# Stage three of a four-layer residual kernel: first tiles read and prepared in the last channels of stage two, and a split last store

## The chip, the cores and the metric

One core of a Trainium2 chip runs the whole program. The time is that of the device for one execution, in microseconds (us), as the median of several runs. Smaller is better.

## The reference, cut to what matters

`x` has shape (B, C, T) = (128, 64, 1024), in fp32. Four layers are added to it one after the other:

```python
x = x + conv(x * mask) * mask        # per channel a causal convolution over t with a kernel of 1024 lags;
                                     # mask: t < length[b]
x = x + einsum('bct,bcd->bdt', x, weights[cond])             # a 64x64 matrix for each b, one of 16
x = x + x @ W2.T + bias2 + (x @ A2[adapter].T) @ B2[adapter].T   # rank 16, one of 32
x = x + x @ W3.T + ((x @ A3[labeler]) @ B3.T) * 0.5              # rank 32, one of 5
```

## The kernel before, in words

The program has three stages. Stage one (to about 210 us) builds constants: the 64 convolution kernels, which it stores to DRAM (`kern_d`), the combined matrix of the two last layers, split into a high and a low part and kept in SBUF (`weights`), and the small low-rank tables, which go to DRAM (`a2_d`, `a3_d`, `b2_d`, `b3_d`, `c_d`).

Stage two works channel by channel, h = 0 to 63. `channel(k, u)` is written for h = 8k + u on each engine. SP loads the lags and the transposed input `xt` three channels ahead and stores the result of the channel (`store_y`, L377): `yo`, 128 batches by 1024, goes to `x1_d`. ACT and DVE split the operands into a high and a low part (`split_high` L625, `split_low` L912). PE convolves (L1071). ACT's `front` (L638) and DVE's `back` (L923) bring the sums of PSUM into `yo[u % 2]`. The block of stage two ends with SP's waits on all stores (L410 and on), and a barrier of all engines.

Stage three works on 64 tiles of two batches each, v = 0 and 1 of a pair n = 0 to 31. A tile is 128 rows (two batches by 64 channels) by 1024. For pair 0, SP loads `x1_in[v]` from `x1_d` and `x_nat[v]` from the input `x` (L1234 on), then the tables of the adapters (`load_tables`, whose row numbers `ids` reads from SBUF, one value at a time), then 22 small pieces (`load_c`, `load_stack` and L1232), then `x_nat` for pair 1 and, in `pair(0)`, `x1_in` for pair 1. POOL copies the 64x64 matrices of each batch into `m_gath[v]` (`gather`, L1274). DVE's `choose` (L1380) overwrites `x1_in` with `x_nat` where t is past the length: two masks (L1391) and one predicated copy (L1396) for each half of a tile. PE's `quarter` (L1522) multiplies a half tile by `m_gath` (L1531), all four quarters through one PSUM bank, from which ACT copies (`take`, L1302). Then PE runs the seven products of a Strassen-like scheme, M1, M5, M2, M4, M6, M3, M7 (`product`, L1544), of 24 pairs of matmuls each (L1560, L1561), with the low-rank parts between them. In the middle of M4 stands `turn(n, 0)` (L1537), a transposition that waits for DVE's `h_rows(n, 0)` (L1437 to L1451).

DVE works in the order in which its code is written. In `pair(n)` it makes the sums and their low parts, then runs `choose(n + 1, 0, 0)` and `choose(n + 1, 0, 1)`, and only then `h_rows(n, 0)`:

```python
if not last_one:
    for half in range(2):
        choose(n + 1, 0, half)
dve.wait_ge(m2_done, n + 1)
h_rows(n, 0)
```

SP, too, works in the written order: what stands behind a long piece of issuing is late by that piece.

## Time and profile before

| | |
|---|---|
| median of 3 runs | 1518.78 us (1516.99 to 1521.23) |
| the profiled execution | 1520.33 us |
| its span, first to last instruction | 1518.6 us |
| mean granted clock of TensorE | 0.988 of full |
| PE busy | 1471.4 us (97%) |
| PE weight load busy | 1418.3 us (93%) |
| DVE busy | 1112.8 us (73%) |
| ACT busy | 630.5 us (42%) |
| POOL busy | 131.9 us (9%) |
| moved by DMA | 276.70 MB, mean 182 GB/s |

The span is shorter than the time of the same execution by 1.73 us, which lie around it. Times in the views are in us from the start of the span. `SPq` and `ACTq` mark the issue of a DMA on that engine. A timeline merges like rows that follow one another (x4). The views leave out buffer numbers: `x_in` is `x1_in`, `x_d` is `x1_d`, `tab` is `tab2` or `tab3`.

### The profile page before, as it was taken

The numbers are of one execution on the slowest core, as the hardware profiler recorded it, in microseconds if no ns is written. First come the engines' busy times: TensorE is split into PE (matmuls) and PEld (weight loads), VectorE is DVE, ScalarE is ACT, GpSimd is POOL, SyncE is SP. The second block draws the span as 40 slices with busy tenths as digits, with TensorE's granted clock in tenths as the row PEclk, the third lists the DMA queues.
The fourth block names the chain that finished last, engine by engine and source line by source line (L and its number), as shares of the span: only waits on it lengthen the run. The fifth ranks groups of instructions, "written<-read, shape, count | busy, mean of one in ns | idle before, by whom it ended". The sixth has DMA issues, their size and how long they took to land.

```text
span 1518.6 us, 34145 instructions
## 1 busy us (share of the span) xinstructions
PE 1471.4 (97%) x10701; PEld 1418.3 (93%) x10701; DVE 1112.8 (73%) x2330; ACT 630.5 (42%) x1249; POOL 131.9 (9%) x197
## 2 busy tenths in 40 slices
PE   6999999999999996999999999999999999999998
PEld 5887889999999995999999999999999999999998
DVE  7864578888888885667777777777777777777774
ACT  3330346665666653334334334334334334334332
POOL 3460210000000000000100100000100100000000
PEclk9999999999999997999999999999999999999999
DMA  9734068888888875445645655655655654644652
GB/s 247 88 135 109 1 204 281 275 277 271 276 270 273 277 252 176 158 143 163 194 145 160 195 144 159 195 146 157 196 147 156 199 144 157 197 146 156 198 146 77
DMA packets 174325, 276.70 MB, mean 182 GB/s; under 512 B 63009, under 2 KB 119725, under 8 KB 171633
## 3 DMA queue, kind: packets, MB, share of 16 engines
q1 hardware_dynamic: 164060, 241.67, 54.0%
q10 hardware_dynamic: 10230, 34.59, 5.7%
q8 instruction: 19, 0.31, 0.1%
q14 instruction: 16, 0.13, 0.0%
HBM read 201.24 MB, written 74.95 MB: 182 GB/s over the span
## 4 chain that ended last, share of the span: by engine, by line
PE 57%; SPq 1%; DMA 1%; issue 1%; DVE 0%; ACT 0%; DVEq 0%; ACTq 0%
PE ps L1560 23%; PE ps L1561 22%; PE ps L1531 8%; PE ps L1568 2%; PE ps L1570 2%; PE ps L1542 1%; DMA out<-y_out 1%; SPq L1185 1%; PE ps L1537 0%; DMA x_nat<-in_x 0%; SPq L1217 0%; DVE weights L1422 0%; DMA tab<-a_d 0%; SPq L1191 0%; ACT a L1305 0%
## 5 line engine op out<-in xcount | busy, mean ns | idle before, releaser
L1560 PE MATMUL ps<-weights,xs 128*128 128x256 f32 x1536 | 396.3, 289 | 0.0
L1561 PE MATMUL ps<-weights,xs 128*128 128x256 f32 (+1 forms) x1536 | 387.6, 292 | 0.0
L1560 PE MATMUL ps<-weights,xa 128*128 128x352 f32 (+1 forms) x1152 | 329.9, 315 | 4.5 <-DVE weights L1422 1.3
L1561 PE MATMUL ps<-weights,xa 128*128 128x256 f32 (+1 forms) x1152 | 324.2, 296 | 0.0
L1561 PEld LDWEIGHTS ps<-weights,xs 128*128 128x128 f32 x1536 | 292.8, 191 | 0.0
L1560 PEld LDWEIGHTS ps<-weights,xs 128*128 128x128 f32 x1536 | 291.8, 190 | 0.0
L1091 PE MATMUL ps<-toep,ut 128*128 128x512 f32 (+2 forms) x1152 | 228.2, 343 | 0.0
L1560 PEld LDWEIGHTS ps<-weights,xa 128*128 128x128 f32 x1152 | 218.1, 189 | 10.1 <-issue 9.8
L1561 PEld LDWEIGHTS ps<-weights,xa 128*128 128x128 f32 x1152 | 219.1, 190 | 0.0
L1091 PEld LDWEIGHTS ps<-toep,ut 128*128 128x128 f32 x1152 | 195.6, 190 | 16.7
L1305 ACT ACTIVATE a<-ps 128x512 f32<-128x512 f32 x128 | 76.5, 598 | 281.6 <-PE ps L1531 281.1
L1531 PE MATMUL ps<-m_gath,x_in 128*128 128x128 f32 x1024 | 139.2, 280 | 13.7 <-DVE x_in L1396 10.4
L1531 PEld LDWEIGHTS ps<-m_gath,x_in 128*128 128x128 f32 x1024 | 128.3, 196 | 14.7 <-DVE x_in L1396 12.2
L1279 POOL COPY m_gath<-mix 64x64 f32 x128 | 54.8, 428 | 824.9 <-PE ps L1531 714.2
L983 PE MATMUL ps<-p,staged 128*128 128x512 f32 x480 | 113.3, 398 | 6.1 <-POOL staged L462 5.5
L629 ACT ACTIVATE ut<-xt 128x896 fp32r<-128x896 f32 x64 | 61.0, 954 | 137.4 <-PE ps L1102 131.4
L983 PEld LDWEIGHTS ps<-p,staged 128*128 128x128 f32 x480 | 92.1, 193 | 26.4 <-issue 6.1
L1396 DVE COPY_PREDICATED x_in<-late,x_nat 128x512 f32<-128x512 uint16 x128 | 95.3, 745 | 19.4 <-DVE late L1391 19.4
L1102 PE MATMUL ps<-toep,ut 128*128 128x256 f32 x768 | 107.4, 289 | 0.0
L1102 PEld LDWEIGHTS ps<-toep,ut 128*128 128x128 f32 x768 | 95.8, 191 | 0.0
L1317 ACT ACTIVATE weights<-tab 128x128 fp32r<-128x128 f32 (+1 forms) x256 | 71.4, 353 | 27.7 <-DVE tab L1413 26.5
L915 DVE TENSOR_TENSOR ut<-xt,ut 128x896 fp32r<-128x896 f32 x64 | 69.9, 1092 | 16.7 <-ACT ut L629 16.7
(223 smaller groups left out, 2204.5 us busy)
## 6 DMA issues: line engine op xcount, KB each, us to landing
lags<-kern_d SPq DMA_DIRECT2D x64, 512.0 KB, 5.7
xt<-in_xt SPq DMA_DIRECT2D x64, 512.0 KB, 6.5
x_d<-yo SPq DMA_DIRECT2D x64, 512.0 KB, 3.2
x_in<-x_d SPq DMA_DIRECT2D x64, 512.0 KB, 6.1
x_nat<-in_x SPq DMA_DIRECT2D x64, 512.0 KB, 3.9
out<-y_out ACTq DMA_DIRECT2D x64, 512.0 KB, 5.4
stack<-b_d SPq DMA_DIRECT2D x130, 128.0 KB, 3.6
tab<-a_d SPq DMA_DIRECT2D x126, 128.0 KB, 2.1
```

The costliest lines, as they stand in the source:

```text
L629: copy(ut[u % 2][:, 0, 0:SPLIT], xt[u % BUFS][:, 0:SPLIT], ACT.Copy).then_inc(ut_hi, 1)
L915: tt(ut[u % 2][:, 1, 0:SPLIT], xt[u % BUFS][:, 0:SPLIT], f(ut[u % 2][:, 0, 0:SPLIT]), ALU.subtract).then_inc(ut_lo, 1)
L983: ins = mm(t[:, cols], staged[n % 2][:, a, c, :], p3[:, c, b, cols], start=c == a == b == 0, stop=c == K8 - 1 and a == 1)
L1091: mm(y[:, half * HB + i * P:(half + 1) * HB], xs[:, a, half * half_t + i, :], tp[:, b, 0:HB - i * P], start=i == a == b == 0, stop=False)
L1102: ins = mm(y[:, to:to + QT], xs[:, a, i, :], tp[:, b, at_col:at_col + QT], start=False, stop=i == half_t - 1 and a == 1)
L1279: ins = nc.gpsimd.tensor_copy(m_gath[v][rows, b * C:(b + 1) * C], mix[rows, bass.ds(s, 1), :].squeeze(1))
L1305: ins = copy(raw[:], mixing, ACT.Copy)
L1317: ins = copy(to, of, ACT.Copy)
L1396: nc.vector.copy_predicated(x1_in[v][:, cols], late[:], x_nat[v][:, cols]).then_inc(chosen[v], 1)
L1531: ins = mm(acc[:, MIX_BANK, i * P:(i + 1) * P], x1_in[v][:, c * P:(c + 1) * P], m_gath[v][:], start=True, stop=True)
L1560: mm(left[0], x_part, left[1], start=first and is_wide, stop=end, skip_group_check=True)
L1561: ins = mm(right[0], x_part, right[1], start=first and is_wide and H_AT[m] > 0, stop=end, skip_group_check=True)
```

## The change

Four things are done.

1. In the last three channels of stage two, between the stores, SP reads the 8 row numbers and loads the first pair's tables; then it loads both `x_nat`; then, when the store of channel 62 has landed, channels 0 to 62 of `x1_in[0]` and `x1_in[1]` in four DMAs of 63 rows; and when `yo` of channel 63 is complete, two DMAs of 2 rows bring channel 63 from that SBUF buffer into the tiles, ahead of the store of channel 63. To make room, tiles of stage three move to addresses that the last channels leave free.
2. ACT's `h_high(0, v)` and DVE's `difference(0)`, `h_low(0, v)` and all eight masks of pair 0 are put before, and around, the work on channel 63. DVE's `memset`s of `hrow`, `hc`, `hs` go behind its first sums.
3. In stage three POOL gathers `m_gath` first and fixes `c_gath` afterwards; the four first quarters go to four PSUM banks in place of one; the waits on the last stores of `x1_d` move to SP, POOL and DVE in stage three.
4. In the last pair, DVE finishes the left half of `y_out[1]` (`y21_added`) before the right half, and the store of `y_out[1]` becomes two, one for each half.

The diff, cut to its core:

```diff
@@ SP, end of stage two
-            for u in range(UNROLL):
+            for u in range(UNROLL - 3):
                 channel(GROUPS - 1, u, loads=False)
-            for u in range(2):
-                sp.wait_ge(x1_stored[u], count_in(GROUPS, 0, 2))
...
+            sp.wait_ge(toep_lo, C - 2)
+            sp.wait_ge(tri_ready, C - 2)
+            for v in range(2):
+                load_tables(sp, v, ids(sp, 0, v, B), ids(sp, 0, v, 2 * B))
+            channel(GROUPS - 1, UNROLL - 3, loads=False)
+            sp.wait_ge(toep_lo, C - 1)
+            sp.wait_ge(tri_ready, C - 1)
+            sp.wait_ge(conv_done, C - 3)
+            for v in range(2):
+                sp.dma_start(x_nat[v][:], x_rows[v]).then_inc(x_landed[v], 16)
+            channel(GROUPS - 1, UNROLL - 2, loads=False)
+            sp.wait_ge(x1_stored[0], count_in(GROUPS, 0, 2))
+            sp.wait_ge(x1_stored[1], count_in(GROUPS, 0, 2) - 16)
+            sp.wait_ge(conv_done, C - 1)
+            for v in range(2):
+                for b in range(2):
+                    sp.dma_start(x1_in[v][b * C:b * C + C - 1], x1_d[2 * v + b, 0:C - 1]).then_inc(first_rows[v], 16)
+            sp.wait_ge(y_front, C)
+            sp.wait_ge(y_back, C)
+            for v in range(2):
+                sp.dma_start(x1_in[v][C - 1::C], yo[1][2 * v:2 * v + 2]).then_inc(first_rows[v], 16)
+            channel(GROUPS - 1, UNROLL - 1, loads=False)
@@ ACT, end of stage two
             for u in range(UNROLL):
+                if u == UNROLL - 1:
+                    for v in range(2):
+                        h_high(act, 0, v)
                 channel(GROUPS - 1, u, ahead=u < UNROLL - 1)
@@ DVE, end of stage two
-            for u in range(UNROLL):
+            for u in range(UNROLL - 1):
                 channel(GROUPS - 1, u, ahead=UNROLL - 1 - u)
+            difference(dve, 0)
+            dve.wait_ge(conv_done, C - 1)
+            for v in range(2):
+                for q in range(4):
+                    nc.vector.tensor_scalar(late_first[:, 2 * v + q // 2, q % 2 * QT:q % 2 * QT + QT], ramp[:], float(q * QT),
+                                            lens_cols[:, v:v + 1], ALU.add, ALU.is_ge).then_inc(masked, 1)
+            h_low(dve, 0, 0)
+            back(GROUPS - 1, UNROLL - 1)
+            h_low(dve, 0, 1)
@@ SP, start of stage three
-            for v in range(2):
-                load_x1(0, v)
-                load_x(0, v)
-            a, l = [None] * 2, [None] * 2
-            a[0], l[0] = ids(sp, 0, 0, B), ids(sp, 0, 0, 2 * B)
-            load_tables(sp, 0, a[0], l[0])
-            a[1], l[1] = ids(sp, 0, 1, B), ids(sp, 0, 1, 2 * B)
+            for u in range(2):
+                sp.wait_ge(x1_stored[u], count_in(GROUPS, 0, 2))
+            a, l = [ids(sp, 0, v, B) for v in range(2)], [ids(sp, 0, v, 2 * B) for v in range(2)]
             sp.wait_ge(c_fixed, 2)
@@ POOL, start of stage three
-            pool.wait_ge(gfixed, 4)
+            pool.wait_ge(gfixed, 2)
...
+            gather(0, 0)
+            gather(0, 1)
+            pool.wait_ge(x1_stored[1], count_in(GROUPS, 0, 2))
+            for v in range(2):
+                nc.gpsimd.tensor_copy(c_gath[v][:], ident[:]).then_inc(gfixed, 1)
@@ DVE, start of stage three
+            def choose_first(v, half):
+                dve.wait_ge(first_rows[v], 48)
+                dve.wait_ge(x_landed[v], 16)
+                dve.wait_ge(masked, 8)
+                cols = slice(half * HB, (half + 1) * HB)
+                nc.vector.copy_predicated(x1_in[v][:, cols], late_first[:, 2 * v + half], x_nat[v][:, cols]).then_inc(chosen[v], 1)
+            for v, half in QUARTERS:
+                choose_first(v, half)
@@ PE, start of stage three
             for q in range(4):
-                quarter(0, q)
+                quarter(0, q, FIRST_BANKS[q])
@@ DVE, last pair
+                if last_one:
+                    dve.wait_ge(u3_copied, n + 1)
+                    tt(halves(y_out[1][:, 0:HB]), halves(y_out[1][:, 0:HB]), of_v, ALU.add).then_inc(y21_added, 1)
                 dve.wait_ge(p_done, n + 1)
                 tt(halves(y_out[1][:, HB:T]), halves(y_out[1][:, HB:T]), of_p, ALU.add).then_inc(y22_added, 1)
@@ ACT, last pair
+                if last_one:
+                    act.dma_start(out_rows[2 * n + 1, :, 0:HB], y_out[1][:, 0:HB]).then_inc(y_stored[1], 16)
+                    act.wait_ge(y22_added, n + 1)
+                    act.dma_start(out_rows[2 * n + 1, :, HB:T], y_out[1][:, HB:T]).then_inc(y_stored[1], 16)
```

How this moves instructions is best seen in each engine's own sequence. SP at the end of stage two, before, from the store of channel 61 (in square brackets the semaphores waited for; `yo_155` is `yo[1]`, `x_in_190` and `x_in_180` are `x1_in[0]` and `[1]`, `tab_1` is `tab2[1]` or `tab3[1]`):

```order
L380 DMA x_d<-yo_155 128x1024 [waits y_back,y_front]
L380 DMA x_d<-yo_146 128x1024 [waits y_back,y_front]
L380 DMA x_d<-yo_155 128x1024 [waits y_back,y_front]
L315 UNCONDITIONAL_BRANCH [waits const_stored,c_stored,a2_stored,b2_stored,a3_stored,x1_stored1,x1_stored0]
L1198 UNCONDITIONAL_BRANCH [waits barrier_Pool_Activation_PE_DVE_SP_release]
L1201 DMA x_in_178<-x_d 128x1024
L1204 DMA x_nat_180<-in_x 128x1024
```

SP at the same place after the change, from the last table load on:

```order
L400 DMA tab_1_188<-a_d 128x256
L500 DMA x_d<-yo_155 128x1024 [waits y_back,y_front]
L545 DMA x_nat_179<-in_x 128x1024 [waits conv_done,tri_ready,toep_lo]
L545 DMA x_nat_195<-in_x 128x1024
L500 DMA x_d<-yo_146 128x1024 [waits y_back,y_front]
L552 DMA x_in_190<-x_d 63x1024 [waits conv_done,x1_stored1,x1_stored0]
L552 DMA x_in_190<-x_d 63x1024
L552 DMA x_in_180<-x_d 63x1024 x2
L556 DMA x_in_190<-yo_155 2x1024 [waits y_back,y_front]
L556 DMA x_in_180<-yo_155 2x1024
L500 DMA x_d<-yo_155 128x1024 [waits y_back,y_front]
```

The tiles' loads have moved ahead of the barrier, and the store of channel 63 now stands behind eight more DMAs. The sequence of SP behind the barrier begins with eight readings of row numbers, then the same 22 pieces and the four loads of pair 1 as before.

DVE around channel 63 after the change (before, the two last pairs of L929, L930 followed each other directly):

```order
L1072 TENSOR_TENSOR yo_146<-ps,shared_in 128x256
L423 TENSOR_TENSOR tab_1_189<-tab_1_189 128x2x64 [waits tab_landed1]
L423 TENSOR_TENSOR tab_1_188<-tab_1_188 128x2x128
L1097 TENSOR_SCALAR late_first<-ramp,lens_cols 128x256 [waits conv_done]
L1097 TENSOR_SCALAR late_first<-ramp,lens_cols 128x256 x7
L432 TENSOR_TENSOR weights<-tab_0_196,weights 128x4x2x16 [waits h_hi0]
L432 TENSOR_TENSOR weights<-tab_0_178,weights 128x4x64
L432 TENSOR_TENSOR weights<-tab_0_196,weights 128x4x2x16
L432 TENSOR_TENSOR weights<-tab_0_178,weights 128x4x64
L1071 TENSOR_TENSOR yo_155<-ps,shared_in 128x256 [waits y_front,conv_done]
L1072 TENSOR_TENSOR yo_155<-ps,shared_in 128x256
```

Fourteen instructions, one of them waiting for a table, now stand between the sums of channel 62 and those of channel 63.

## Rows read from the trace of the kernel before

**Rows 1.** The chain of waits, 550 to 665 us (start us, us, what)
```profile
584.65 4.57 DMA x_nat<-in_x
...
637.67 1.78 SPq L1185
```

**Rows 2.** PE's timeline (start us, us, engine line, operation, count, [idle before <-releaser])
```profile
578.64 1.67 PE L1102 MATMUL ps<-toep,ut 128*128 128x256 f32 x12
590.74 2.08 PE L1531 MATMUL ps<-m_gath,x_in 128*128 128x128 f32 x8 [10.43 <-DVE x_in L1396]
...
603.55 0.55 PE L1560 MATMUL ps<-weights,xa 128*128 128x256 f32 x1 [1.28 <-DVE weights L1422]
...
618.01 0.27 PE L1537 MATMUL ps<-ident,hrow 128*128 128x128 f32 x1
```

**Rows 3.** Windows: us, then PE, PEld, DVE, ACT, POOL busy, PEclk, DMA share, GB/s
```profile
585.00:586.00 1.00, 0.00 (x0) 0.00 (x0) 0.00 (x0) 0.00 (x0) 0.43 (x3) 0.76 0.35 106
...
588.00:589.00 1.00, 0.00 (x0) 0.00 (x0) 0.00 (x0) 0.00 (x0) 0.42 (x2) 0.50 1.02 410
...
597.00:598.00 1.00, 1.00 (x5) 1.00 (x6) 0.85 (x4) 0.00 (x0) 0.00 (x0) 0.50 1.01 205
...
609.00:610.00 1.00, 1.00 (x7) 1.00 (x7) 0.00 (x0) 0.18 (x1) 0.00 (x0) 0.79 1.09 430
```

**Rows 4.** SP's timeline: its DMA issues
```profile
563.92 17.59 SPq L380 DMA_DIRECT2D x_d<-yo  x4
584.26 0.34 SPq L1201 DMA_DIRECT2D x_in<-x_d  x1
...
588.73 0.34 SPq L1190 DMA_DIRECT2D tab<-a_d  x1
...
593.12 0.34 SPq L1210 DMA_DIRECT2D c_gath<-c_d  x1
...
603.67 0.84 SPq L1204 DMA_DIRECT2D x_nat<-in_x  x2
604.56 0.91 SPq L1201 DMA_DIRECT2D x_in<-x_d  x2
610.25 0.35 SPq L1190 DMA_DIRECT2D tab<-a_d  x1
```

**Rows 5.** DVE's timeline around the end of stage two and pair 0
```profile
580.69 0.41 DVE L930 TENSOR_TENSOR yo<-ps,shared_in 128x256 f32<-128x256 f32 x1
...
602.24 2.31 DVE L1422 TENSOR_TENSOR weights<-tab,weights 128x128 fp32r<-128x128 f32 x8
...
612.55 0.48 DVE L1391 TENSOR_SCALAR late<-ramp,lens_cols 128x256 uint16<-128x256 int16 x2 [0.88 <-DMA x_in<-x_d]
...
614.71 0.74 DVE L1396 COPY_PREDICATED x_in<-late,x_nat 128x512 f32<-128x512 uint16 x1 [0.15 <-DVE late L1391]
616.53 0.42 DVE L1446 COPY hrow<-ps 64x48 f32<-64x48 f32 x2 [1.08 <-PE ps L1561]
616.99 0.42 DVE L1450 TENSOR_TENSOR hrow<-hrow,ps 64x48 f32<-64x48 f32 x2
```

**Rows 6.** POOL's timeline at the start of stage three
```profile
585.25 0.23 POOL L1284 MEMSET c_gath<- 128x64 f32 x2
...
587.18 0.23 POOL L1279 COPY m_gath<-mix 64x64 f32 x1 [0.48 <-issue]
```

**Rows 7.** An earlier pause of PE: its timeline
```profile
83.31 2.07 PE L983 MATMUL ps<-p,staged 128*128 128x512 f32 x5 [1.82 <-POOL staged L462]
```

**Rows 8.** Windows of 0.5 us after that pause (columns as in rows 3)
```profile
87.00:87.50 0.50, 0.50 (x4) 0.41 (x3) 0.00 (x0) 0.00 (x0) 0.50 (x1) 0.82 0.27 115
```

**Rows 9.** ACT's timeline, the last output stores
```profile
1514.13 0.35 ACTq L1362 DMA_DIRECT2D out<-y_out  x1
1515.32 0.35 ACTq L1364 DMA_DIRECT2D out<-y_out  x1
```

**Rows 10.** Windows of 1 us at the very end (columns as in rows 3)
```profile
1515.00:1516.00 1.00, 0.00 (x0) 0.00 (x0) 0.29 (x1) 0.00 (x0) 0.00 (x0) 1.00 1.01 410
```

270 lines of the change are left out of this document (140 added, 130 removed).

## The prediction

> **What bounds the kernel now.** The page comes first: PE is busy for 97% of the span, so time can only be won where PE stands still or runs at its lower clock. The list of waits and the chain of waits then tell where that is. Nearly all of stage three after pair 1 is PE behind PE; the one long hole is the passage from stage two to stage three, where the chain leaves PE for a store, a load of `x_nat` (4.57 us) and the first choice [rows 1]. PE's timeline gives its size: the last matmul of channel 63 ends at 580.31, the first quarter starts at 590.74, 10.43 us later [rows 2]. The windows show what that costs beyond itself: the granted clock, 0.76 in the window 585 to 586 and 0.50 in the later ones, falls there, five us after PE stopped, that is from 2.4 to 1.2 GHz, and comes back in 609 to 610 [rows 3]. The four quarters run at the lower clock, 2.08 us for eight matmuls, with waits for ACT between them, and M1 starts only at 603.55, behind the tables' low parts [rows 2]. From the end of stage two to M1 it is 23.2 us.
>
> The reader should then not stop at PE. SP's timeline for the same stretch [rows 4] is an unbroken row of issues from 584.26 to 605.47, and its last two, the loads of `x1_in` for pair 1, are what DVE waits for at 612.55, in the middle of pair 0 [rows 5]. DVE stands 0.88 us there; behind it in DVE's order are the second choice (to 615.45), then a wait of 1.08 us for M2, then `h_rows` (to 617.41), and PE's `turn` at 618.01, which PE reaches in that moment [rows 2, 5]. So in pair 0 today two chains arrive together at the turn: PE's own products, and SP, loads, DVE. The change shortens the first by some 10 us. What it does to the second decides the time.
>
> **Part one, the first wait.** SP stores channel 60 at 563.92 to 564.27 [rows 4]. Eight readings of row numbers and eight table issues follow. From 588.73 to 593.12 SP did four issues and four readings, 4.39 us [rows 4]; twice that is 8.8, so the store of channel 61 goes out at 573.4 and not at 569.9. Nobody is hurt: its buffer is wanted by ACT only for channel 63, at 577. Both `x_nat` go out to 574.7, the store of 62 at 575.4, when DVE has closed it. These four transfers are 2.1 MB; at 410 GB/s, the rate of such 4 KB rows in a full window [rows 3], they take 5.1 us from 574.3 and the last has landed at about 580.0. Then the four 63-row loads (580.05 to 581.8 at 0.43 each), two small ones, and the store of channel 63 from 582.6 instead of 581.17.
>
> How fast the 63-row loads are no row of this trace shows. They are 1.03 MB: 2.5 us at the 410 GB/s of the full tiles, 5.0 us at the 205 GB/s at which the short pieces of `stack` fill the DMA engines [rows 3]. I take the middle, 3.75, since they are long rows like the first, but an odd number of them; both ends stay for the range. They start at 581.45 (a load's data began 1.4 us after its issue at 584.26), end at 585.2, and the two small pieces behind them land at 585.8. POOL begins when the barrier opens, about 0.4 us after SP's last issue, 583.4; two memsets take 0.5, and from the end of the memsets to the first finished `m_gath` it was 585.48 to 587.41, 1.93 [rows 6]. That is 585.8, too, and DVE's choice ends at 586.6. PE's first quarter thus starts at 586.6, 4.1 us earlier, in a bank of its own each; at the lower clock the four end at 594.9, and M1 starts there, its tables being ready. Against 603.55 that is 8.7 us won at this point.
>
> The cover of the preparation: on DVE `difference`, eight masks (two are 0.48) and half of `h_low` (all eight 2.31) [rows 5] stand between the sums of 62 (575.35) and those of 63, and need the tables, landed at about 575.5; 0.6 + 1.9 + 1.2 ends at 579.3, ahead of 580.35. I cost it at nothing; if the tables are over 1 us later, every further us delays the sums of 63 and all behind them.
>
> **Part two, the second chain.** SP in stage three may begin when the store of 63 has landed. It queues behind the 63-row loads: 585.2, plus 1.3 for its 0.52 MB, plus 0.5 to the semaphore, 587.0 (585.8 to 588.3 between the two prices), against 583.8 before. Then eight readings (605.47 to 610.25, 4.8) and the 22 pieces (593.12 to 603.67, 10.55) [rows 4]. `x_nat` of pair 1 is issued at 602.35 instead of 603.67, 1.3 earlier (2.5 to 0.0). Nothing shortens the way from there: the choice starts at 611.25, the second ends at 614.15, the wait for M2 is gone, `h_rows` takes 0.9, and the turn comes at 615.15. That is 2.9 us before 618.01 (4.1 to 1.6). PE took 14.46 from M1 to the turn, 5.9 of it at half rate [rows 2, 3], so 11.5 at full clock, and is there at about 606. **Of the 8.7 us won, some 6 are lost again in a new wait of about 9 us in the middle of M4.**
>
> **Part three, the clock.** A stop of 9 us is as long as today's. The earlier pause of only 1.82 us before 83.31 cost it too: the clock is at 0.82 in the window from 87.0, in which it comes back [rows 7, 8], 3.9 us after PE resumed; M1 at 603.55 had to wait 5.9 [rows 3]. At 0.50 a matmul takes twice its time, so behind the turn 1.5 to 3 us are lost; I take 2.2, a little above half of 3.9. The Trainium skill (TensorE: Matmul & The Clock Gate, Part 1) says the default state is throttled and activity releases it; by that the new idle stretch brings the lower clock back, and the granted clock here agrees (0.50 after 585, five us after PE stopped). Without it the sum would be 2.2 better.
>
> **Part four, the end.** Before, the two stores go out at 1514.13 and 1515.32 [rows 9], and the DMA engines are full from 1515 on [rows 10]: together 1.05 MB at 410 GB/s, 2.6 us without a gap. The first store is not earlier now, the bytes are the same, and the halves are issued by 1514.7 and 1515.3. The tail is bound by the bytes: 0 (0.2 lost to 0.6 won).
>
> **Sum.** 2.9 at the turn, less 2.2 for the clock, 0 for the tail: 0.7 us won, between 2.6 won (4.1 less 1.5) and 1.4 lost (1.6 less 3). Pair 1 and later keep their order. The profiled execution had 1520.33, of which 1518.6 are the span; it would become 1519.6. The median of the runs was 1.55 lower: **1518.1 us**. A measurement of this kernel can tell about 0.3%, 4.6 us, from no change.
>
> **Rivals.**
> *The new wait stays, the clock does not fall, and the loads are at their fast price.* Then 4.1 us are won: 1514.7. For it speaks that the first pause left the clock up for five us [rows 3]; against it the length of the new pause. Chance 0.17, a quarter of it beyond 0.3%.
>
> *The second chain is not bound to SP*, the turn waits for nobody, and all of part one arrives: 8.7 us, 1510.1. It would need `x1_in` of pair 1 some 8 us earlier. Against it stands the count of SP's issues, which is the same. 0.10.
>
> *The 63-row loads use fewer DMA engines.* Nine sixteenths of 410 is 231 GB/s, 4.5 us for 1.03 MB: the store of 63 lands at 587.8, 0.75 later than in my sum, and the small pieces at 586.6. All of it arrives at the turn: 0.7 less 0.75, 1518.8. The mechanism here would be that a load of 63 rows leaves seven of the sixteen engines idle. The Trainium skill (DMA: Bandwidth & Descriptors, Why a DMA increments its semaphore by 16 and not by 1) says that a hardware-issued DMA is spread over the largest number of engines up to 16 that divides its slowest dimension, which for 63 is 9. No row before shows it. 0.10.
>
> *Slower: SP's readings of row numbers in their new place are slow the first time.* Each us of the tables beyond 1 delays the sums of 63, the store of 63 and SP's stage three one for one, and the readings in stage three are the same code written anew. SP had pieces of 1.78 us on that line the first time through its loop, against about 0.6 [rows 1]. Four such in each of the two places cost about 3.7 in stage two beyond the cover of 1, and 4.7 in stage three: 1518.1 + 8.4 less 1 is 1525.5. It decides from the point where the store of 63 lands after 592. Against it: the readings of stage three before were also run for the first time, at 4.39 us for four with four issues. 0.09.
>
> My own case has 0.54. **Chances:** faster by over 0.3%: 0.10 + 0.04 = 0.14; within: 0.54 + 0.13 + 0.10 = 0.77; slower: 0.09. The range takes the bounds of the sum (1516.2 to 1520.2), the first rival at 1514.7 and the spread of the runs, some 2 us, above: 1514.5 to 1521.5. What is left out is the second rival and the last, 0.19.
>
> **What would show it.** PE's first quarter at about 586.6, M1 at about 595; a wait of PE before `turn` of some 9 us, released by DVE's `hrow`, that was not there before; DVE waiting for `x1_in` of pair 1 for 8 us or so before the choice; granted clock 0.50 twice, once around 586 and once around the turn; SP's `x_nat` of pair 1 at 602 or so; pair 1 starting within 2 us of its old 634.8. I am wrong if PE passes the turn without a wait, if channel 63 closes later than 581.1, or if the last store ends over 1 us earlier after `p_done` than the 5.2 us it took.

## The result, and the profile after

| | before | after |
|---|---|---|
| median of 12 runs | 1517.37 us | 1521.69 us |
| range of the runs | 1515.25 to 1521.23 | 1520.15 to 1524.49, and 1613.64 |
| the profiled execution | 1520.33 us | 1523.72 us |
| its span | 1518.6 us | 1522.0 us |
| mean granted clock | 0.988 | 0.990 |

The ratio is 1.0027, with a 95% interval of 1.0019 to 1.0036. The run of 1613.64 us was disturbed (a granted clock of 0.85 in place of 0.99) and stays out of the ratio; without it the median after is 1521.60. The change costs 4.3 us between the medians, where I had forecast 0.7 us won, and 1521.69 lies just above the range of 1514.5 to 1521.5. The forecast of 1518.1 stood on a median of 3 runs, 1518.78; on the 1517.37 of the 12 runs the same sum would have given 1516.7.

All times that are compared below are taken from the end of the last matmul of channel 63, 580.31 before and 579.57 after, so that what stages one and two do by themselves drops out. Nothing of the change hides in that: from the end of channel 59 to the end of channel 63 PE takes 23.01 us in both kernels, so the work that was moved into the last channels does not slow the convolutions. PE's timeline of the changed kernel, the lines that answer to [rows 2]:

```profile
577.90 1.67 PE L1253 MATMUL ps<-toep,ut 128*128 128x256 f32 x12
590.56 6.32 PE L1590 MATMUL ps<-m_gath,x_in 128*128 128x128 f32 x32 [10.98 <-DVE x_in L1471]
...
596.63 0.36 PE L1619 MATMUL ps<-weights,xa 128*128 128x256 f32 x1
...
617.73 0.47 PE L1596 MATMUL ps<-ident,hrow 128*128 128x128 f32 x1 [7.71 <-DVE hrow L1501]
```

The hole before the first quarter has not become shorter (10.99 us after 10.43). The four quarters no longer wait for ACT between them, and M1 no longer waits for DVE's low parts, so M1 starts 17.06 us after the end of stage two, against 23.24: 6.2 us won there. Then comes a wait that was not there before, 7.71 us in front of the `turn`, and the turn is 0.46 us later than before (38.16, was 37.70). The two causes stand in SP's timeline, the lines that answer to [rows 4]:

```profile
573.20 0.37 SPq L500 DMA_DIRECT2D x_d<-yo  x1
573.67 1.23 SPq L545 DMA_DIRECT2D x_nat<-in_x  x2
574.99 0.41 SPq L500 DMA_DIRECT2D x_d<-yo  x1
582.00 1.41 SPq L552 DMA_DIRECT2D x_in<-x_d  x4
583.51 1.16 SPq L556 DMA_DIRECT2D x_in<-yo  x2
584.77 0.37 SPq L500 DMA_DIRECT2D x_d<-yo  x1
596.05 0.34 SPq L1287 DMA_DIRECT2D c_gath<-c_d  x1
...
606.68 0.84 SPq L1308 DMA_DIRECT2D x_nat<-in_x  x2
607.57 0.91 SPq L1278 DMA_DIRECT2D x_in<-x_d  x2
```

Between the store of channel 62 (574.99) and the four 63-row loads (582.00) SP stands, and again between the store of channel 63 (584.77) and its readings. The chain of waits names both, and the wait for pair 1 behind them (start us, us, what):

```profile
574.99 6.99 DMA x_d<-yo
...
584.77 6.35 DMA x_d<-yo
591.20 0.45 SPq L394
...
607.57 6.46 DMA x_in<-x_d
```

DVE's timeline shows the ends of the two chains, the first choice and the choice for pair 1, each behind a wait of over 8 us (before, the second one was 0.88, [rows 5]):

```profile
579.61 0.42 DVE L1071 TENSOR_TENSOR yo<-ps,shared_in 128x256 f32<-128x256 f32 x1 [1.36 <-PE ps L1253]
...
589.77 2.73 DVE L1471 COPY_PREDICATED x_in<-late_first,x_nat 128x512 f32<-128x512 uint16 x4 [8.33 <-DMA x_in<-yo]
...
614.05 0.48 DVE L1458 TENSOR_SCALAR late<-ramp,lens_cols 128x256 uint16<-128x256 int16 x2 [8.19 <-DMA x_in<-x_d]
```

The windows (us, then busy share and count of PE, PEld, DVE, ACT, POOL, then PEclk, DMA share, GB/s; before in [rows 3]) show the granted clock fall twice, to 0.50 of full, that is 1.2 GHz:

```profile
582.00:583.00 1.00, 0.00 (x0) 0.00 (x0) 0.00 (x0) 0.00 (x0) 0.00 (x0) 0.57 0.18 29
583.00:584.00 1.00, 0.00 (x0) 0.00 (x0) 0.00 (x0) 0.00 (x0) 0.00 (x0) 0.50 0.47 119
...
596.00:597.00 1.00, 1.00 (x11) 1.00 (x10) 0.00 (x0) 0.98 (x2) 0.00 (x0) 1.00 0.00 0
...
613.00:614.00 1.00, 0.00 (x0) 0.00 (x0) 0.00 (x0) 0.00 (x0) 0.00 (x0) 0.50 1.02 406
622.00:623.00 1.00, 1.00 (x7) 1.00 (x7) 0.86 (x3) 0.00 (x0) 0.00 (x0) 0.50 0.00 0
623.00:624.00 1.00, 1.00 (x10) 1.00 (x10) 0.00 (x0) 0.66 (x2) 0.00 (x0) 0.95 0.00 0
```

The second fall is new and costs time behind the turn. Worked out from the windows, the clock stands at its lower level for 13.7 us around the hole and for 10.2 us around the turn; before it was one stretch of 23.9 us. By "the fourth quarter of pair 0" I mean the last quarter that PE works in `pair(0)`, which already belongs to the tiles of pair 1. From the turn to this quarter it was 15.71 us before (618.01 to 633.72) and is 18.22 (617.73 to 635.95): 2.51 lost. Pair 1 gives part of that back. From the fourth quarter of pair 0 to that of pair 1 it is 28.68 us, where it was 29.91 (before, PE waited 1.1 us for ACT's `y_out` in it, and in the changed kernel it does not). The mark used below is this fourth quarter of pair 1, the first line for before, the second for after, from the chains of waits:

```profile
663.63 0.89 PE ps L1531 x8
```

```profile
664.63 0.89 PE ps L1590 x8
```

Counted from the end of stage two that is 83.32 and 85.06: **1.74 us lost in the passage**, 0.46 at the turn and 2.51 behind it, less 1.23 in pair 1. The size of this loss depends on the execution that it is measured against. e4 and e6 below are kernels of the old kind that run the same instructions up to the mark: e4 has its turn at 37.72 and its mark at 83.33, as before, but e6 has them at 36.80 and 82.53. Against e6 the loss is 2.5 us, and the turn is 1.4 us late. The span grew by 3.4 us: 1.74 up to the mark and 2.19 in later pairs (below), 0.2 at the end, less 0.74 by which the end of stage two came earlier. The end of the program is the same: the last DMA ends at 1522.0, 31.05 us after the last fourth quarter (1490.95); before it was 30.84.

### The profile page after: what moved, and what is told of

It reads as the page before. It is cut to its first block, busy times and chain, and to the rows that moved or that the text cites. A ratio compares the mean times of both kernels' runs of the same rounds, so it can differ in the third digit from the quotient of the medians.

```text
span 1522.0 us, 34157 instructions
## 1 busy us (share of the span) xinstructions
PE 1470.2 (97%) x10701; PEld 1418.3 (93%) x10701; DVE 1111.0 (73%) x2330; ACT 628.8 (41%) x1249; POOL 123.7 (8%) x197
## 4 chain that ended last, share of the span: by engine, by line
PE 90%; DVE 3%; issue 2%; POOL 2%; SPq 2%; DMA 2%; ACT 0%; DVEq 0%; POOLq 0%
PE ps L1619 23%; PE ps L1620 23%; PE ps L1242 13%; PE ps L1590 7%; PE ps L1134 6%; PE ps L1253 6%; PE ps L1233 3%; PE ps L1627 2%; PE ps L1629 2%; PE ps L1245 2%; PE ps L1601 1%; DMA x_d<-yo 1%; PE ps L1120 1%; POOL staged L601 1%; SPq L394 1%
## 5 line engine op out<-in xcount | busy, mean ns | idle before, releaser
L1351 POOL COPY m_gath<-mix 64x64 f32 x128 | 45.9, 358 | 835.3 <-PE ps L1590 702.0
```

The costliest lines, as they stand in the source:

```text
L1351: ins = nc.gpsimd.tensor_copy(m_gath[v][rows, b * C:(b + 1) * C], mix[rows, bass.ds(s, 1), :].squeeze(1))
```

## The experiments

Fourteen experiments were run, two of them a kernel once more (e14 and e7b). In the table all places are us after the end of stage two in the profiled execution of each; "mark" is the fourth quarter of pair 1; the ratio is to the kernel before, measured on the same chip, with its 95% interval. The marks scatter, too. One program run twice gave 85.06 and 85.33 (changed, e14) but also 75.25 and 73.68 (e7, e7b), and the old code up to the mark gave 83.32, 83.33 and 82.53 (before, e4, e6). So differences of some 1.5 us between two marks prove nothing by themselves; the mechanism is read from the waits and from larger steps of the marks, the worth from the ratios.

| kernel | first quarter | M1 | turn (PE's wait there) | mark | ratio |
|---|---|---|---|---|---|
| before | 10.43 | 23.24 | 37.70 (0) | 83.32 | 1 |
| changed | 10.99 | 17.06 | 38.16 (7.71) | 85.06 | 1.0027 [1.0019, 1.0036] |
| e14, changed again | 11.55 | 17.21 | 38.43 (7.84) | 85.33 | 1.0025 [1.0012, 1.0037] |
| e1, pair 1 first | 11.08 | 16.94 | 30.17 (0) | 76.25 | 0.9963 [0.9950, 0.9977] |
| e2, readings ahead | 12.17 | 17.52 | 36.15 (5.24) | 82.37 | 1.0011 [1.0002, 1.0020] |
| e3, 48 and 15 rows | 12.18 | 17.48 | 38.00 (7.14) | 86.00 | 1.0025 [1.0015, 1.0036] |
| e4, before with new places | 10.37 | 23.17 | 37.72 (0) | 83.33 | 1.0001 [0.9992, 1.0010] |
| e5, before, pair 1 first | 10.43 | 23.24 | 36.66 (0) | 83.63 | 1.0001 [0.9992, 1.0010] |
| e6, before with new tail | 10.47 | 23.27 | 36.80 (0) | 82.53 | 1.0001 [0.9992, 1.0010] |
| e8, e1 and three waits | 12.57 | 18.08 | 31.31 (0) | 77.24 | 0.9968 [0.9959, 0.9977] |
| e11, `x_nat` behind | 9.24 | 14.24 | 33.88 (6.25) | 81.04 | 0.9984 [0.9974, 0.9993] |
| e12, and 48 rows | 9.00 | 14.30 | 34.64 (6.95) | 81.91 | 0.9991 [0.9982, 1.0001] |
| e7, combined | 10.24 | 16.48 | 29.57 (0) | 75.25 | 0.9956 [0.9942, 0.9969] |
| e7b, combined again | 9.86 | 14.90 | 28.12 (0) | 73.68 | 0.9935 [0.9921, 0.9949] |
| e10, and gathers early | 8.74 | 14.05 | 27.27 (0) | 74.75 | 0.9927 [0.9914, 0.9941] |
| e13, and `x_nat` later | 6.89 | 12.91 | 26.13 (0) | 72.44 | 0.9937 [0.9921, 0.9954] |

### Is it SP's second chain that holds the turn?

**e1** puts the four loads for pair 1 ahead of the 22 pieces, and changes nothing else of the changed kernel:

```diff
+            for v in range(2):
+                sp.wait_ge(chosen[v], 2)
+                sp.dma_start(x_nat[v][:], x_rows[2 + v]).then_inc(x_landed[v], 16)
+            sp.wait_ge(mixed, 4)
+            for v in range(2):
+                load_x1(1, v)
             for v in range(2):
                 load_c(v, a[v], l[v])
...
-                for v in range(2):
-                    load_x1(n + 1, v)
+                if not (isinstance(n, int) and n == 0):
+                    for v in range(2):
+                        load_x1(n + 1, v)
```

> The changed kernel, with SP's four loads for pair 1 (x_nat, x1_in) issued ahead of the 22 small pieces in place of behind them. Theory S (SP's queue holds the turn of pair 0): PE's wait of 7.7 us before the turn goes, and the second stretch at granted clock 0.50 with it, 2.5 us more; with it the kernel is 8 to 10 us faster than the change, some 1512 to 1514. The pieces now land by 610, before the adapters want them. Theory L (the loss sits in the longer period of the later pairs, from the new places of the tiles): the wait may go, but the period of 28.53 us against 28.40 stays, and the time stays some 2 us above what theory S gives. If the wait at the turn comes from another thing than x1_in of pair 1, nothing changes: 1521.

Measured: the turn comes at 30.17 without a wait, 8.0 us earlier than in the changed kernel, with the first quarter and M1 where they were. PE's timeline of this kernel:

```profile
589.29 6.11 PE L1594 MATMUL ps<-m_gath,x_in 128*128 128x128 f32 x32 [11.07 <-DVE x_in L1475]
608.38 0.27 PE L1600 MATMUL ps<-ident,hrow 128*128 128x128 f32 x1
```

The matmul of the turn takes 0.27 us again, where it took 0.47 in the changed kernel: the clock does not fall a second time. The mark is 8.8 us earlier and the ratio 0.9963, 6.4 thousandths or 9.7 us below that of the changed kernel. So the 6.2 us won at M1 were there all along, and the new wait and its clock took them and more. The median of 1511.97 is what theory S had given, 1512 to 1514.

**e5** makes the same edit in the kernel before:

> The kernel before, with its four loads for pair 1 ahead of the 22 small pieces, and nothing of the change. Theory S2 (in the kernel before, PE's own products and SP's chain meet at the turn; only the change makes SP's chain the longer): PE has no wait to lose there, and the time is that of before within 0.1%. Rival (the order of SP alone is worth what the change with the new order won, 5.6 us): 1512.

The ratio is 1.0001. The turn came at 36.66 in place of 37.70, which is no effect of the edit, as e6 without it had 36.80; the mark is not earlier. Before the change, PE's own products arrived at the turn when SP's chain did, and the order of SP's loads was worth nothing. It became worth 0.6% by the change.

**e2** lets SP read the eight row numbers ahead of its wait for the store of channel 63, so that 4.85 us of readings lie beside the store:

```diff
+            a, l = [ids(sp, 0, v, B) for v in range(2)], [ids(sp, 0, v, 2 * B) for v in range(2)]
             for u in range(2):
                 sp.wait_ge(x1_stored[u], count_in(GROUPS, 0, 2))
-            a, l = [ids(sp, 0, v, B) for v in range(2)], [ids(sp, 0, v, 2 * B) for v in range(2)]
```

> The changed kernel, with SP's eight readings of row numbers ahead of its wait for the store of channel 63 in place of behind it. Theory S: what stands behind that wait moves one for one, by 4.8 us, so PE's wait at the turn falls from 7.7 to about 3, and the time by 4.8 us, or more if the clock then stays up: 1515 to 1517. If the loads of pair 1 are bound by the DMA engines and not by SP's issuing, less than 2 us.

The wait at the turn shrinks to 5.24 us, not to the 3 that I expected, and the turn comes at 36.15, 2.0 earlier and not 4.8. The ratio is 1.0011, a median of 1519.30 where I had expected 1515 to 1517. The trace shows where the rest went. SP's first piece goes out 1.8 us after the landing of the store of 63 (592.39 to 594.15), where it was 4.9 (591.12 to 596.05), so 3.2 of the 4.85 are saved; in the 1.8 us POOL fixes `c_gath` (592.53 to 593.81), which waits for the same store and for which SP waits. The store itself landed 0.9 us later in this execution. The second chain is confirmed from its other end, with this piece of POOL's as the next thing on it.

### What made the two stores land late?

**e3** cuts each 63-row load into 48 and 15 rows:

```diff
-                    sp.dma_start(x1_in[v][b * C:b * C + C - 1], x1_d[2 * v + b, 0:C - 1]).then_inc(first_rows[v], 16)
+                    for r0, r1 in ((0, 48), (48, C - 1)):
+                        sp.dma_start(x1_in[v][b * C + r0:b * C + r1], x1_d[2 * v + b, r0:r1]).then_inc(first_rows[v], 16)
...
-                dve.wait_ge(first_rows[v], 48)
+                dve.wait_ge(first_rows[v], 80)
```

> The changed kernel, with each load of 63 rows made of one of 48 and one of 15. Theory N (63 rows keep only nine of the sixteen DMA engines busy, as the share of 0.5 to 0.6 from 583 to 586 and again from 587.5 to 590 suggests): the share goes to 0.9 or more, the four loads and the store of channel 63 take some 2 to 3 us less, less 1.7 us for four more issues; the store lands 0.5 to 1.5 us earlier and the time falls by as much. Rival (the rows are slow since they were written just before): the share and the landing stay, and the time rises by the issues, up to 1.7 us.

No gain: ratio 1.0025, turn at 38.00, where I had expected 0.5 to 1.5 us. But the store of channel 63, issued at 587.73, now lands 3.16 us after its issue, where it took 6.35. It went out 3 us later: 2.1 of that is the price of four more issues (eight loads took SP 3.49 us, four took 1.41), the rest came with the store of 62, which landed 7.95 us after its issue in this execution. From the issue of the first load to the landing of the store it is 8.0 us with the loads cut, and 9.1 without, for the same bytes. So of the 3.2 us won at the landing the issues take two thirds, and the 1.1 that is left is too small for the ratios to show.

**e11** takes the two loads of `x_nat` from ahead of the store of 62 and puts them behind the store of 63. It leaves first that store, then the 63-row loads alone on the DMA engines:

```diff
...
-            for v in range(2):
-                sp.dma_start(x_nat[v][:], x_rows[v]).then_inc(x_landed[v], 16)
             channel(GROUPS - 1, UNROLL - 2, loads=False)
...
             channel(GROUPS - 1, UNROLL - 1, loads=False)
+            for v in range(2):
+                sp.dma_start(x_nat[v][:], x_rows[v]).then_inc(x_landed[v], 16)
```

> The changed kernel with the two loads of x_nat behind the store of channel 63 in place of ahead of the store of 62. It isolates two sizes of my sum. First the landing of the store of 62 (6.99 us after its issue in the changed kernel). Theory R: it was late because it shared the DMA engines with 1.05 MB of x_nat; alone it lands 2.5 to 3.5 us after its issue, at about 578. Rival S: something else is slow there (the store itself, or a wait that I don't see); it still takes over 5 us. Second the four 63-row loads, now alone on the DMA engines: theory of nine engines: DMA share 0.5 to 0.6 at about 230 GB/s for 4 us or more. Rival: 1.0 and 350 to 410 GB/s for 2.5 to 3 us. The store of 63 is then issued at 581 to 582 and lands at 585 to 586.5; the first quarter waits for x_nat (+9.5 to +11), the turn comes at +32 to +34, with a wait of 2 to 4 us, and the time is 3 to 5 us below the changed kernel, ratio about 0.9995.

**e12** does the same with 48 rows in the early loads, the other 15 behind the store of 63, ahead of `x_nat`:

> As the last, with 48 rows in place of 63 in the four early loads, and rows 48 to 62 in four more behind the store of channel 63. Theory of nine engines for 63 rows and all sixteen for 48: in the windows in which the 48-row loads are alone, the DMA share is 0.9 to 1.0 at 350 GB/s or more, and their 0.79 MB take about 2 us in place of 4.5; the store of 63 lands 1 to 2.5 us earlier after its issue than with the 63 rows. Rival (such loads right behind a store are slow whatever their rows): share 0.5 to 0.6 and 230 GB/s again, 3.4 us, and the store of 63 lands as late after its issue.

The view of the tile `x_d` gives for each kernel the DMAs' shortest, median and longest time from issue to landing. The changed kernel's three stores (61, 62, 63):

```profile
L500 SPq DMA_DIRECT2D x_d<-yo x3: 368/371/406, 573.2 to 584.8; - x3
DMA to landing us min/median/max: 3.1/6.3/7.0
```

e11, in this window the stores of 62 and 63:

```profile
L500 SPq DMA_DIRECT2D x_d<-yo x2: 342/356/370, 573.3 to 580.3; - x2
DMA to landing us min/median/max: 2.9/4.0/5.0
```

e12, all three:

```profile
DMA to landing us min/median/max: 2.7/2.9/3.0
```

In the changed kernel the DMA engines had a full share between the issue of the store of 62 and its landing, and for two us of it about half the rate of 410:

```profile
576.00:577.00 1.00, 1.00 (x7) 0.87 (x7) 1.00 (x7) 1.00 (x6) 0.00 (x0) 1.00 0.96 193
577.00:578.00 1.00, 1.00 (x10) 1.00 (x9) 1.00 (x5) 0.59 (x2) 0.00 (x0) 1.00 0.99 233
```

So the store of 62 takes 2.9 us without `x_nat` ahead of it and 7.0 with it: that cause is shown. The store of 63, behind `x_nat` no more but behind loads of the first rows, takes 5.0 with 63 rows and 3.0 with 48. e11's windows while the 63-row loads are in flight, before the next store goes out at 580.33:

```profile
578.00:579.00 1.00, 0.19 (x2) 0.00 (x0) 0.77 (x3) 0.00 (x0) 0.00 (x0) 1.00 0.54 213
579.00:580.00 1.00, 0.00 (x0) 0.00 (x0) 1.00 (x4) 0.00 (x0) 0.00 (x0) 1.00 0.55 188
```

and e12's with the 48-row loads:

```profile
580.00:581.00 1.00, 0.43 (x4) 0.23 (x2) 0.53 (x2) 0.00 (x0) 0.00 (x0) 1.00 1.05 279
581.00:582.00 1.00, 0.00 (x0) 0.00 (x0) 1.00 (x5) 0.00 (x0) 0.00 (x0) 1.00 0.92 213
582.00:583.00 1.00, 0.00 (x0) 0.00 (x0) 0.29 (x1) 0.00 (x0) 0.00 (x0) 0.73 0.55 135
```

The share of the DMA engines is 0.54 and 0.55 with 63 rows, with nothing else to do, and 0.92 to 1.05 with 48. Nine of sixteen is 0.56. This is my third rival's mechanism. The Trainium skill (DMA: Bandwidth & Descriptors, Why a DMA increments its semaphore by 16 and not by 1) has a hardware-issued DMA spread over the largest number of engines up to 16 that divides the slowest dimension of both its sides, which is nine for 63. The trace agrees, with 0.54 to 0.58. The rate with 48 rows, 213 to 279 GB/s at a full share, is not the 410 of the full tiles, nor the 350 that I had expected of e12. Small loads are slow for another reason, too, and no run tells which.

The 5.0 and 3.0 us of the store do not measure the number of engines alone. The 48-row loads carry a quarter fewer bytes, and they were over before the store's data began: in e12 the share is down to 0.55 in 582 to 583, and the store went out at 582.62. The loads of e3, too, were nearly over when its store began. The fairer size is e3's, 8.0 against 9.1 us with the same bytes ahead of the store, and there SP's issues, not the engines, set when the store begins.

In the changed kernel the loads were not over. The store went out at 584.77, and its windows show what follows:

```profile
586.00:587.00 1.00, 0.00 (x0) 0.00 (x0) 0.00 (x0) 0.00 (x0) 0.00 (x0) 0.50 1.05 340
587.00:588.00 1.00, 0.00 (x0) 0.00 (x0) 0.00 (x0) 0.00 (x0) 0.05 (x1) 0.50 0.61 152
588.00:589.00 1.00, 0.00 (x0) 0.00 (x0) 0.00 (x0) 0.00 (x0) 0.22 (x2) 0.50 0.51 201
589.00:590.00 1.00, 0.00 (x0) 0.00 (x0) 0.23 (x1) 0.00 (x0) 0.29 (x2) 0.50 0.51 209
```

The share is full for about one us and then falls back to 0.51 until all has landed. By an estimate from the rows: 1.03 MB / 9 is 0.114 MB for each, and a sixteenth of the store 0.033 more, 0.147 MB at 410/16, or 25.6 GB/s, is 5.7 us. The loads were issued at 582.00, and a load's data began 1.4 us after its issue in the kernel before: 583.4, and 589.1 for the end. The last window with more than a few packets is 589 to 590, so the estimate is up to 1 us short; the first two windows, 582 to 584, carried only 29 and 119 GB/s.

e11 also shows what the order of the two loads is worth in the changed kernel: the turn comes 4.3 us earlier and the ratio is 0.9984, just below 1. It missed my 2 to 4 us of wait at the turn (6.25), because M1 came 2.8 us earlier, too.

### The other parts of the change

**e4** is the kernel before with the tiles at the places of the changed one:

> The kernel before, with the tiles of stage three at the places that the change gives them, and nothing else. Theory L: the later pairs take 28.53 us in place of 28.40, and the kernel is 2 to 4 us slower than before. Rival (the period has nothing to do with the places, and goes with how PE's stream happened to start, or with the run): the same time as before within 0.1%, with a period of 28.40 in most pairs.

**e6** is the kernel before with the last pair's new order and the split store:

> The kernel before, with the last pair's two parts of the change alone: y21 added before y22, and the last store in two halves. Theory T (the last 1.05 MB fill the DMA engines): no difference, under 0.5 us, and the end comes 5 to 5.5 us after the last matmul. Rival: half of the last store goes out 0.6 us earlier, and the end is 0.6 to 1.2 us earlier.

Both have a ratio of 1.0001 with intervals of 0.0009 to either side. Neither the places nor the tail cost or win anything that can be measured. The 2 to 4 us that theory L gave the places did not come.

### The longer period of the later pairs

In the profile of the changed kernel, two of three later pairs (22 of 30) took 28.53 us in place of 28.40, and from the mark to the last fourth quarter it was 2.2 us longer than before. The last two fourth quarters in the chain of waits of the changed kernel:

```profile
1462.42 0.89 PE ps L1590 x8
...
1490.95 0.89 PE ps L1590 x8
```

**e8** (e1 with three more waits on PE, fulfilled long before, that move its code) was to tell whether the place of PE's code makes this, and **e14**, the changed kernel once more, whether the program does at all:

> The kernel with the loads of pair 1 first, with three semaphore waits more on PE ahead of its first quarters, all of them long fulfilled, so that PE's loop over the pairs stands at the places of the kernel before. Theory A (the longer period of 28.53 us comes with the place of PE's instructions, three waits fewer in the change): the period is 28.40 in most pairs, and the time some 3 to 4 us less, 1508 to 1509. Rival (it comes with the relative timing of the engines, or of SP, DVE and ACT code): the period stays 28.53 in most pairs, and the time stays at 1512.

> The changed kernel itself, once more. Of the 3.4 us that its span had more than before's, 2.2 came from pairs behind pair 1 with a period of 28.53 in place of 28.40 us, in two pairs of three. Theory: the longer period is a matter of the single execution. Then this profile will show another share of such pairs than two thirds (none, as in the kernel with x_nat behind the last store, or half), and if it shows fewer, its span will be shorter by 0.13 us for each one, while first quarter (+11.0), M1 (+17.1) and turn (+38.2, with a wait of 7 to 8 us) stay. Rival: it belongs to this program; then again two of three. The median of the runs will be 1520 to 1522.5 again.

e8 had the longer period in two of three pairs, as e1 had it in nearly all. e14 had it in none, with the same program:

```profile
1461.26 0.89 PE ps L1590 x8
...
1489.66 0.89 PE ps L1590 x8
```

Its span is 1520.5, and first quarter, M1, turn and mark are those of the first profile within 0.6 us. The same program can thus run with and without the longer period: e6, of the old kind, had it in most of its pairs, and e11, of the new kind, in none. It explains 2.2 us of the difference between two profiles. Whether it explains some of the difference between the medians is open: of the profiles of the old kind one in four had it in several pairs (e6), of those of the new kind eight in twelve, and one profile of each kernel can't tell whether the change makes it more frequent. e14's median is again above that of before by 4.3 us, though its profile has none of it; the mark explains 1.7 to 2.8 of them, by the execution it is measured against.

### Versions that beat both

**e7** combines e1, e2 and rows 0 to 47 ahead of the store of 62's landing; **e7b** is the same kernel on another chip. **e10** moves POOL's memsets and gathers of `m_gath` for pair 0 into stage two. **e13** moves `x_nat` behind the rows:

```diff
@@ e7, SP
+            sp.wait_ge(conv_done, C - 1)
+            for u in range(2):
+                sp.wait_ge(x1_stored[u], count_in(GROUPS, 0, 2) - 32)
+            for v in range(2):
+                for b in range(2):
+                    sp.dma_start(x1_in[v][b * C:b * C + 48], x1_d[2 * v + b, 0:48]).then_inc(first_rows[v], 16)
...
@@ e10, POOL, end of stage two
+            pool.wait_ge(toep_hi, C)
+            pool.wait_ge(toep_lo, C)
+            for v in range(2):
+                nc.gpsimd.memset(m_gath[v][:], 0.0).then_inc(gfixed, 1)
...
@@ e13, SP
                     sp.dma_start(x1_in[v][b * C + 48:b * C + C - 1], x1_d[2 * v + b, 48:C - 1]).then_inc(first_rows[v], 16)
+            for v in range(2):
+                sp.dma_start(x_nat[v][:], x_rows[v]).then_inc(x_landed[v], 16)
```

> The changed kernel with the loads of pair 1 first, the row numbers read ahead of the wait, and rows 0 to 47 of the first tiles loaded before the store of channel 62 has landed, rows 48 to 62 after it. Theory S and N: the last rows land some 3 us earlier, PE's first quarter is bound by POOL's m_gath instead (about 2 us earlier than in the change), and the time is 1 to 2 us below that of the order alone (1511.97), 1510 to 1511. If the clock stays up since PE's pause is shorter, up to 4 us more.

> The combined kernel once more, beside the one with POOL's gathers early, to compare them on one chip: ratio to before 0.994 to 0.997 again. If the longer period of 28.53 us per pair in some pairs is a matter of the execution and not of the program, its share among the pairs (about half last time) will be another one in this profile.

> The changed kernel with pair 1 first, the readings ahead and rows 0 to 47 early, as in the combined kernel, and now also the memsets and copies of m_gath for pair 0 in POOL's program of stage two, behind the last reader of fold, whose place they take. In the combined kernel PE's first quarter waited for POOL (m_gath complete, 10.24 us after the end of the convolutions), while DVE's first choice had ended at about 7.7 to 8. Theory: POOL was the last thing on that path, and the rest of the chain has slack: first quarter at +7.5 to +8.5, M1 at +13.5 to +14.5, turn without a wait of over 1 us at +26.5 to +27.5, span and time 2 to 3 us below the combined kernel. Rival 1: ACT and DVE's work between the quarters and M1, or the turn's chain over SP, comes last: M1 moves, the turn stays at +29 to +29.6, time as the combined kernel. Rival 2: POOL's copies disturb DVE's or ACT's last sums of stage two, the convolutions end later and the gain is lost.

> The combined kernel with POOL's gathers early, and now also the two loads of x_nat behind rows 48 to 62 in place of ahead of the store of channel 62. There the store of 62 landed 8 us after its issue, and rows 48 to 62 went out only at 583.73, the first choice began at 587.66, +7.95 after the end of the convolutions. Theory: what holds the first quarter is the landing of the store of 62 behind x_nat on the DMA engines; without it ahead it lands at about 578 (2.9 us after its issue, as alone), rows 48 to 62 go out at 578 to 579.7, and all of the first tiles has landed at 584 to 585.5. First quarter at +5.5 to +7, M1 at +11 to +13, turn at +24.5 to +26.5, ratio to before 0.990 to 0.992. Rival: x_nat, now last, comes as late as the rows did; first quarter at +8.5 to +9.5 and the time as before this step, 0.993. Second rival: the turn then waits again for x1_in of pair 1, since SP's stage three hangs on the store of 63; the gain ends at that chain.

The first quarters of e7, e10 and e13 from PE's timelines:

```profile
588.69 6.48 PE L1599 MATMUL ps<-m_gath,x_in 128*128 128x128 f32 x32 [10.23 <-POOL m_gath L1360]
```

```profile
588.45 5.56 PE L1606 MATMUL ps<-m_gath,x_in 128*128 128x128 f32 x32 [8.73 <-DVE x_in L1487]
```

```profile
585.75 6.27 PE L1606 MATMUL ps<-m_gath,x_in 128*128 128x128 f32 x32 [6.88 <-DVE x_in L1487]
```

The releaser changes from POOL to DVE, and the wait shrinks from 10.23 to 8.73 and 6.88. But the marks (73.68 to 75.25, then 74.75, then 72.44) and the ratios (0.9956 and 0.9935, then 0.9927, then 0.9937) move less. e7 expected 1 to 2 us more than the order of the loads alone gave, and its ratio can't be told from those of e1 and e8. e10 met its places and not its 2 to 3 us: it was 1.1 us ahead of e7b at the first quarter, and nothing that can be measured in time. e13 met its places, too, and missed its 0.990 to 0.992. Its profile shows where part of the gain goes, as waits of PE after the turn, the list of waits from 600 to 690:

```profile
PE ps L1643 <- ACT y_out L1436: 1.7, 1, 1.7
PE ps L1635 <- ACT y_out L1418: 1.3, 1, 1.3
```

e7b has 2.1 us of such waits, e13 3.0 and e10 4.1 (one for `stack` among them). PE now meets ACT's copies and SP's pieces. In e13 the granted clock also falls once more, right behind the mark, after the wait of 1.7 us (PE resumed at 650.56):

```profile
653.00:654.00 1.00, 1.00 (x6) 1.00 (x6) 0.65 (x2) 0.32 (x1) 0.28 (x2) 0.50 0.91 86
654.00:655.00 1.00, 1.00 (x6) 1.00 (x6) 1.00 (x3) 0.63 (x1) 0.74 (x1) 0.50 0.76 246
```

The next pair takes 29.82 us there, against 28.26 in e10 and in e7b: 1.6 us lost, more than the 1.24 by which e13's mark is ahead of e7b's. e10 had a wait as long at the same place and kept its clock, so this is no fixed price of e13's edit. The best ratios, 0.993 to 0.994, are some 10 us better than before and 14 better than the change; e7b, e10 and e13 can't be told apart.

## Why the prediction was wrong

The bound, the two chains and the cancelling were right; two landings were too short, and both lie on the path. They are the step that failed, points 1 and 2 here. The prediction's places are in the time of the kernel before, in which stage two ends 0.74 us later; the measured places below stand as the trace has them, and 0.74 is added to them where a difference is given.

1. **Part one, the landing of the store of 62**, *"the last has landed at about 580.0"*: wrong, 581.98, 2.7 us late. I had put all 2.1 MB at 410 GB/s. The engines moved 193 to 233 GB/s for two us of it; e11 shows that `x_nat` ahead of the store is the cause (2.9 us without), not why `x_nat` moved so slowly.
2. **Part one, the 63-row loads**, *"I take the middle, 3.75"*: the choice of the middle was wrong, and the third rival right in its mechanism as far as the shares show it. That rival put the loads at 4.5 us and the store's delay at only 0.75, as it, too, let the store's bytes go over all sixteen engines at once. *"587.0 (585.8 to 588.3 between the two prices)"* for the store of 63 became 591.12, outside both bounds: from the first load's issue to that landing it was 9.1 us and not 6.95. So SP's second chain began 4.9 us later than in the sum, 2.7 by point 1 and 2.2 by this one. Had the nine engines been priced as in the rival, 0.75 of the 2.2 would have been covered.
3. **PE's first quarter**, *"thus starts at 586.6"*: 590.56. M1 at 594.9 and 8.7 us won: 596.63, and 6.2 won. The four quarters took 6.1 us, not 8.3. I had taken four times the 2.08 us of a quarter that stands alone, but in one row the matmuls start every 0.213 us at the lower clock, which gives about 7.0 for 32 of them; the other 0.9 is the clock, which came back for the last nine.
4. **Part two.** Readings 4.8 and pieces 10.55: 4.85 and 10.6, right. `x_nat` of pair 1 went out at 606.68 in place of 602.35, 5.1 us late. From there to the choice of pair 1 it was 7.4 us, not the 8.9 of before, so not all of the lateness arrived: the turn was 0.46 later than before and not 2.9 earlier. The sign of the sum hung on this.
5. **The new wait** of about 9 us: 7.71, right in kind, place and releaser. The turn was later than in the sum, but so was PE: it stopped 13.4 us after M1's start and not 11.5, 1.3 of it in a wait for ACT's `y_out` that the sum had at nothing. **Part three, the clock**, 2.2 lost: 2.51 between the turn and the fourth quarter. The size is near by a price too short: the clock came back 5.4 us after PE resumed, not 3.9. Pair 1 began 2.9 us later than before, where the list of signs had 2. In e1, without the wait, the clock stays up at the turn. The first rival (the wait stays, the clock does not fall) did not happen.
6. **Part four, the tail**, 0: right (e6).
7. **The cover of the preparation** on DVE: right. DVE's sums of channel 63 start 0.04 us after PE's end (579.61), as before (580.35; the line in [rows 5] is the second of the two). The store of channel 61, forecast at 573.4, went out at 573.20, 0.5 late by the common mark; the sum had 564.27 + 8.8, which is 573.1.
8. **The slower rival**, SP's readings slow the first time: did not happen (573.20 again, and 4.85 us for eight in stage three). Its own sum took the cover of 1 us off twice: 3.7 and 4.7 make 1526.5 and not 1525.5. **The second rival**, the turn not bound to SP: refuted by e1.

With the measured terms in it, my sum gives 0.46 + 2.51 lost at the fourth quarter of pair 0. Pair 1 then gives 1.0 to 1.2 back, which I had not looked at: PE's wait for ACT in it (1.1 us) is gone, or 0.2 in e14. That leaves 1.7 to 2.0 us lost, 1519.1 to 1519.4 on the median of 12 runs; against e6's mark it would be 2.5 to 2.8. **What stays open:** the medians differ by 4.3 us in both measurements, and some 2 us of that lie in no stretch that the profiles can tell apart. The end of stage two alone came at 577.79 to 580.43 among the profiled executions, and before and e6, with the same code up to there, differ by 2.52. The longer period may have a part in it.

## What to carry to other kernels

When two chains arrive together at a wait, an edit that shortens one of them is worth nothing until the other is shortened, too, and may lose what a second idle stretch costs in clock; here the order of four loads was worth nothing before the change and 0.6% after it. Before a load is put ahead of a store on whose landing something waits, ask what it does to that landing: here 1.05 MB of `x_nat` took it from 2.9 to 7.0 us. The engines that a load occupies count as well as its bytes. What is not urgent goes behind, and a cut into more loads pays its issues (2.1 us for four more here, of 3.2 won at the landing). A price between two bounds that lies on the path should not be taken from the middle if a rule says which bound it is near.

## What the runs showed that I had not expected

- A load of 63 rows holds the DMA engines at a share of 0.54 to 0.58, and a store of 128 rows behind four of them lands 6.35 us after its issue. Where loads of 48 rows were over or nearly so when the store's data began, it was 3.0 and 3.16.
- Loads in stretches with a full share moved anything from 193 to 422 GB/s, with packets of the same 4 KB. The slow ones came while stores and loads ran together, or with loads of 48 rows. The cause is open.
- The granted clock fell at different distances after PE had stopped: between 580 and 581 in e11, where PE had stopped at 578.19, and only after 584 in e13, where it had stopped at 578.86. e13's window:

```profile
583.00:584.00 1.00, 0.00 (x0) 0.00 (x0) 0.00 (x0) 0.00 (x0) 0.00 (x0) 1.00 1.03 414
584.00:585.00 1.00, 0.00 (x0) 0.00 (x0) 0.04 (x1) 0.00 (x0) 0.00 (x0) 0.53 1.04 422
```

- The clock also fell, for 3.4 us, after a wait of PE of only 1.65 us in e13, and did not after one of 1.75 us in e10.
- The same program runs its pairs at 28.40 or 28.53 us, and stays at one of them for many pairs of an execution (e14 against the first profile).
